# Layer 1 of a two-layer decoder: ten shared heads moved beside the last tile's chain, fp8 rounding moved to earlier steps

## The reference

```python
qkv = x @ W_qkv.T + b_qkv                       # causal attention, 16 heads of 16, B = 8, S = 128
x4 = layernorm(x + (softmax(mask(q k^T / 4)) v) @ W_out.T + b_out)
q = fq_sym((x4 @ Wq + bq) * 0.25)               # per row and head: round(q / s) * s, s = max|q| / 127
attn = fq_unsigned(softmax(q k^T))              # every head: all 1024 rows against all 1024 keys
x5 = layernorm(x4 + (attn @ v) @ Wp + bp)
wq = w.astype(float8_e4m3fn)                    # gate, up and down weights
out = layernorm(x5 + (silu(x5 @ wq_gate * s) * (x5 @ wq_up * s)) @ wq_down * s)
```

## Time and profile before

| | us |
|---|---|
| median of 3 runs | 1417.89 (1417.55 to 1419.35) |
| profiled execution, its own time | 1417.26 |
| its span | 1415.5 |
| first pass, steps 2 to 8 | about 1004.5 to 1124.8 |
| from there to head 0's reduction | 1124.8 to 1144.6 |
| SP's transposes, first and last start | 1147.5 and 1347.8 |
| feed-forward part to the end | 1347 to 1415.5 |

### The profile page before, as it was taken

How to read it: one execution, slowest core, us unless ns; L and a number is a source line. 1 busy time by engine, 2 the same in 40 slices (tenths; PEclk the granted TensorE clock), 3 DMA queues, 4 the chain that set the end, 5 groups by cost and what they waited for, 6 DMA issues and landing times.

```text
span 1415.5 us, 24455 instructions
## 1 busy us (share of the span) xinstructions
PE 1237.8 (87%) x9108; PEld 850.1 (60%) x9113; DVE 1046.5 (74%) x2349; ACT 675.3 (48%) x1286; POOL 135.1 (10%) x223
## 2 busy tenths in 40 slices
PE   6979999999999999999899999989899746677686
PEld 3747666766766766766676676656777623333344
DVE  6778578588677767858857775744888788889877
ACT  2336435434533633643553363442444358878751
POOL 2210010010011001002001100000000011111101
PEclk9989999999999999999999999999999955555588
DMA  7331002000100200200010013000300179989910
GB/s 240 154 105 63 12 12 66 13 1 16 63 12 16 62 12 12 66 12 5 26 49 12 12 63 120 20 23 24 78 8 9 31 124 167 173 151 181 166 23 30
DMA packets 176117, 86.06 MB, mean 61 GB/s; under 512 B 138240, under 2 KB 170368, under 8 KB 175744
## 3 DMA queue, kind: packets, MB, share of 16 engines
q1 hardware_dynamic: 174848, 84.13, 25.3%
q10 hardware_dynamic: 1152, 0.36, 0.1%
HBM read 43.57 MB, written 5.24 MB: 34 GB/s over the span
## 4 chain that ended last, share of the span: by engine, by line
PE 63%; DVE 19%; ACT 6%; issue 6%; DMA 5%; POOL 1%; SPq 0%; DVEq 0%; POOLq 0%; ACTq 0%
PE ps_t L1890 12%; PE ps_p L1874 11%; PE ps_s L2123 8%; PE ps_o L2040 5%; DMA w_moe<-w_moe 4%; PE ps_o L2030 4%; PE ps_o L1955 4%; PE ps_o L2123 3%; PE ps_p L1932 3%; DVE probs L1275 2%; ACT w_moe L1116 2%; PE ps_s L1932 2%; PE ps_o L1959 2%; DVE w_moe L1778 2%; DVE row_max L1281 1%
## 5 line engine op out<-in xcount | busy, mean ns | idle before, releaser
L1890 PE MATMUL ps_t<-ident,probs 128*128 128x128 f32 x1072 | 170.3, 280 | 28.5 <-ACT probs L1065 8.0
L925 ACT ACTIVATE probs<-probs 128x512 f32<-128x512 f32 x184 | 115.6, 628 | 136.6 <-DVE probs L1275 136.6
L1890 PEld LDWEIGHTS ps_t<-ident,probs 128*128 128x128 f32 x1072 | 123.2, 142 | 78.1 <-issue 37.9
L887 ACT ACTIVATE probsT<-ps_t 128x512 f32<-128x512 f32 x232 | 136.5, 589 | 64.0 <-PE ps_t L1890 63.8
L2123 PE MATMUL ps_s<-w_moe,xbT 128*128 128x352 f32 x352 | 122.1, 471 | 0.0
L1874 PE MATMUL ps_p<-w_qkv,xinT 128*128 128x512 f32 (+1 forms) x240 | 104.8, 560 | 11.4 <-DMA xinT<-in_xT 7.6
L2399 PEld LDWEIGHTS ps_p<-vals,w_moe 128*128 128x128 f16 x1024 | 37.2, 105 | 97.7 <-DMA w_moe<-w_moe 76.4
L831 POOL TENSOR_TENSOR rms<-mean_sq,neg_half 128x8 f32<-128x8 f32 x40 | 67.1, 1679 | 267.3 <-DVE mean_sq L1309 267.3
L887 ACT ACTIVATE bigT<-ps_t 128x512 f32<-128x512 f32 (+1 forms) x128 | 69.0, 553 | 33.3 <-PE ps_t L1890 31.4
L2399 PE MATMUL ps_p<-vals,w_moe 128*128 128x16 f16 x1024 | 48.2, 176 | 38.6 <-DMA w_moe<-w_moe 37.9
L2123 PEld LDWEIGHTS ps_s<-w_moe,xbT 128*128 128x128 f32 x352 | 64.0, 194 | 22.1 <-issue 1.5
(11 more groups left out here) (342 smaller groups left out, 2736.5 us busy)
## 6 DMA issues: line engine op xcount, KB each, us to landing
w_out<-in_wT_out SPq DMA_DIRECT2D x8, 2048.0 KB, 8.4
w_moe<-in_wT_gu SPq DMA_DIRECT2D x1, 5632.0 KB, 17.6
w_moe<-in_wT_down SPq DMA_DIRECT2D x1, 2816.0 KB, 10.2
keys<-keys2T SPq DMA_DIRECT2D x8, 256.0 KB, 2.0
keys2T<-keys SPq DMA_DIRECT2D x4, 512.0 KB, 10.4
w_moe<-w_moe SPq DMA_TRANSPOSE x128, 3.3
w_qkv<-in_wT_qkv SPq DMA_DIRECT2D x3, 512.0 KB, 4.9
w_qkv<-in_wT_qkv SPq DMA_DIRECT2D x1, 1536.0 KB, 8.3
```

What stands on the lines that cost most here:

```text
L887: nc.scalar.activation(dst, src.bitcast(BF16) if dst.dtype == BF16 else src, ACT.Copy)\
L925: nc.scalar.activation(probs[:, at % 4, :], probs[:, at % 4, :], ACT.Exp).then_inc(L0.exped, 1)
L1890: ins = nc.tensor.transpose(dst[:, i * P:(i + 1) * P], src(i), ident_b[:] if bf else ident[:])
```

## The change

- `STEPS_A` becomes 9: steps 9 and 10 are gone, and what they did for tile 7 stands in the loop over the heads.
- The nine fp8 pieces go to steps 1 to 8: one a step, and two in step 5.
- Heads 0 to 9 (`HEAD_START`) alternate between `ps_s` and `ps_o` and wait for exp u - 2, while `ps_t` serves tile 7's turns; from head 10 on the three pairs go round from `ps_t`, with the wait for exp u - 3.
- PE: behind head 0's scores the turn `o1` of tile 7 and `qs` of tile 6, behind head 1's the out1 projection, behind head 3's the turn `x4`, behind head 4's the q2 projection, behind head 8's the turn `qs` of tile 7. DVE, ACT and POOL have their parts at matching heads; `queries` is split into three.
- SP: the swaps of tiles 3, 4, 6 and 7 are issued inside its loop at u = 10, behind the wait for exp 10 and ahead of transpose 10.
- The first gate and up block waits for exp 125 instead of 126, the second for 126 instead of 127.

```diff
-STEPS_A = TILES + 3
+STEPS_A = TILES + 1
+HEAD_START = 10
...
-ROUND_FROM = 2
-assert ROUND_FROM + len(PIECES) <= STEPS_A
+ROUND_AT = {i: PIECES[i - 1:i] for i in range(1, 5)} | {5: PIECES[4:6]} | {i: PIECES[i:i + 1] for i in range(6, 9)}
...
-            return (ps_s, ps_o, ps_t)[u % 3]
+            return (ps_s, ps_o)[u % 2] if u < HEAD_START else (ps_t, ps_s, ps_o)[(u - HEAD_START) % 3]
...  SP
-            sp.wait_ge(L1.proj, L1.p.done(0, ("q2", LAST)))
-            for t in (3, 4, 6, 7):
-                swap_halves(t)
             for u in range(TILES * H1):
                 sp.wait_ge(exp2, u + 1)
+                if u == HEAD_START:
+                    sp.wait_ge(L1.proj, L1.p.done(0, ("q2", LAST)))
+                    for n in (3, 4, 6, 7):
+                        swap_halves(n)
...  POOL
-            for t in range(TILES):
+            for t in range(LAST):
                 power1(N4, t)
...
+                if u == 1:
+                    power1(N4, LAST)
...  ACT
+            turned("o1", LAST, lane_of(LAST).attT, D)
+            turned("qs", LAST - 1, stackTs[:, LAST - 1])
             for u in range(TILES * H1):
                 t, h = u // H1, u % H1
+                if u == 3:
+                    turned("x4", LAST, lane_of(LAST).x4T, D)
+                if u == 8:
+                    turned("qs", LAST, stackTs[:, LAST])
                 act.wait_ge(max2_ready, u + 1)
...  DVE
+            take(LAST)
             for u in range(TILES * H1):
...
+                if u == 1:
+                    norm_in(N4, LAST, "out1", xins[LAST % XINS], more=b_out1)
+                if u == 2:
+                    norm_out(N4, LAST, x4s[:, LAST])
+                if u == 4:
+                    queries_scaled(LAST)
+                if u == 5:
+                    queries_rounded(LAST)
+                if u == 6:
+                    queries_stacked(LAST)
...  PE
-                    pe.wait_ge(exp2, HEADS - 1 + b)
+                    pe.wait_ge(exp2, HEADS - 2 + b)
...
-                    if u >= 3:
+                    if 2 <= u < HEAD_START:
+                        pe.wait_ge(exp2, u - 1)
+                    if u > HEAD_START:
                         pe.wait_ge(exp2, u - 2)
...
+                    if u == 0:
+                        pe.wait_ge(taken1, TILES)
+                        turn("o1", LAST, lambda k: lane_of(LAST).att[:, k * P:(k + 1) * P], KD)
+                        queries_turned(LAST - 1)
+                    if u == 1:
+                        turned("o1", LAST)
+                        project(L1, ("out1", LAST), lane_of(LAST).attT, w_out1, 0, D)
+                    if u == 3:
+                        pe.wait_ge(N4.x_ready, TILES)
+                        turn("x4", LAST, lambda k: x4s[:, LAST, k * P:(k + 1) * P], KD)
+                    if u == 4:
+                        turned("x4", LAST)
+                        project(L1, ("q2", LAST), lane_of(LAST).x4T, w_q2, 0, D)
+                    if u == 8:
+                        queries_turned(LAST)
```

More of the change, by code:

```diff
@@ L215, in transposes1 @@
     keys = []
-    for i in range(STEPS_A):
+    for i in range(STEPS_A + 2):
         p, s, q, r = at_a(i)
@@ L508, in shared_scores @@
         def shared_scores(u):
-            return (ps_s, ps_o, ps_t)[u % 3]
+            return (ps_s, ps_o)[u % 2] if u < HEAD_START else (ps_t, ps_s, ps_o)[(u - HEAD_START) % 3]
         def block_banks(b):
-            return ps_s if b % 2 == 0 else ps_o
+            return (ps_s, ps_o)[b % 2]
         def last_sums(d):
@@ L1687, in add_bias, with queries_scaled @@
                                         heads(b_qkv1[:, D * i:D * (i + 1)], H1), ALU.add).then_inc(L1.proj_taken, 1)
-            def queries(q):
+            def queries_scaled(q):
                 lane, q2s = lane_of(q), q2ss[:, q]
@@ L1696, in queries, with queries_rounded @@
                 link1(nc.vector.tensor_reduce(q2s[:, 0, :], heads(q2, H1), X, ALU.max, apply_absolute_value=True))
+            def queries_rounded(q):
+                q2s, q2 = q2ss[:, q], lane_of(q).q2
                 link1(nc.vector.tensor_scalar(q2s[:, 0, :], q2s[:, 0, :], 1.0 / 127.0, 1e-8, ALU.mult, ALU.max))
@@ L1701, in queries, with queries_stacked @@
                 link1(nc.vector.tensor_scalar(q2, q2, ROUND, ROUND, ALU.add, ALU.subtract))
+            def queries_stacked(q):
+                lane, q2s = lane_of(q), q2ss[:, q]
+                q2 = lane.q2
                 link1(nc.vector.tensor_scalar(q2, q2, 127.0, -127.0, ALU.min, ALU.max))
@@ L1706, in queries @@
                 ins.then_inc(q2_ready, 1)
+            def queries(q):
+                queries_scaled(q)
+                queries_rounded(q)
+                queries_stacked(q)
             for i in range(STEPS_A):
@@ L1736, in _ @@
                     nc.vector.tensor_scalar(vals2[:].bitcast(FP16), values, 127.0, -127.0, ALU.min, ALU.max).then_inc(v_quantised, 1)
-                if ROUND_FROM <= i < ROUND_FROM + len(PIECES):
-                    round_fp8(*PIECES[i - ROUND_FROM])
+                for piece in ROUND_AT.get(i, ()):
+                    round_fp8(*piece)
                 if q is not None:
@@ L2328, in _, with queries_turned @@
             pe.wait_ge(v_quantised, 3)
-            pe.wait_ge(L1.shifted, TILES * G1)
-            pe.wait_ge(taken1, TILES)
             HEADS = TILES * H1
+            def queries_turned(n):
+                pe.wait_ge(q2_ready, n + 1)
+                turn("qs", n, lambda j: lane_of(n).stack[:, 2 * j:2 * j + 2, :].rearrange("p a b -> p (a b)"), 8, bf=True)
             def out_turn(n):
@@ L2377, in _ @@
                     own, other = (w.rearrange("p (a b) -> p a b", a=8) for w in (stackTs[:, t], swapped[t]))
-                    if u == 2:
+                    if u == 0:
+                        pe.wait_ge(L1.shifted, TILES * G1)
+                    if u == 1:
+                        pe.wait_ge(taken1, TILES)
+                    if u == HEAD_START:
                         turned("qs", LAST)
-                    if u >= 3:
+                    if 2 <= u < HEAD_START:
+                        pe.wait_ge(exp2, u - 1)
+                    if u > HEAD_START:
                         pe.wait_ge(exp2, u - 2)
```

## The result

The changed kernel took 1421.43 us (median of 7 runs, 1419.47 to 1424.81) against 1417.73 of the kernel before on the same chip: ratio 1.0029, 95% interval [1.0018, 1.0039]. By the medians it is 3.7 us slower. (The ratios here are estimated from all the runs of both kernels, and need not be the quotient of the medians, which is 1.0026 here.) That lies inside the range of the prediction (1413.5 to 1422.5), but the likeliest direction, "no change", was wrong: the loss is just over the 0.2% that can be told apart.

What follows compares the result with a forecast made beforehand. The prediction took a DVE, ACT and PE chain to pace the first pass and SP's issue of transposes the second from head 6 to 28. Pieces +5.5, earlier transpose 10 -4.0, tail -0.6 gave +0.9: 1418.5 us, "no change", range 1413.5 to 1422.5.

Steps and rivals of the forecast that it cites:

- the term for the fp8 pieces: First pass: an added piece lengthens DVE's list by 3.03 us in step 1 and 2.49 in step 5, +5.5 us.
- rival 1: Swaps between transposes 9 and 10 cost 1.28 us each, 10.2 instead of 5.0, giving 1423.7 us; chance 0.15.
- The swaps: Second pass, between transposes 9 and 10: eight swaps hold SP, which paces the pass, for 5.0 us.
- Rival 2: Second pass: SP's list has room, so the swaps are covered, 5.0 us less, 1413.5 us; chance 0.12.
- The head start: Handover to the second pass: heads run beside tile 7's work, so exp 10 ends 6.6 us earlier.
- Rival 1's neighbour: Handover: a head start some 3 us shorter than worked out, giving 1421.5 us; chance 0.06.
- the shift stays until the end: Second pass from head 10: SP is back to back, so transpose 10's shift, 4.0 us earlier, lasts to the pass's end.
- The tail: End of the second pass: the first gate and up block needs exp 125, not 126, and starts earlier, -0.6 us.
- Rival 3: First pass: other slack swallows both added fp8 pieces, 5.5 us less, 1413.0 (one of them, about 1415.7); chance 0.08.
- Rival 4: Handover: the clock stays high for two projections and four groups of turns, saving some 2.5 us, 1416.0; chance 0.09.

Runs made afterwards that it cites:

- E3: The changed kernel with twelve useless matmuls on PE ahead of the turn `o1` in steps 2 and 6: 1417.17 us, ratio 1.0005 to the kernel before.
- E5: The kernel before with only its eight swaps moved between transposes 9 and 10: 1421.19 us, ratio 1.0026.
- E2: The changed kernel with the swaps of tiles 3, 4, 6, 7 moved ahead of SP's wait for exps 30, 46, 62, 78: 1416.65 us, ratio 0.9999.
- E7: The changed kernel with the first two gate and up blocks waiting for one exp more, as before: 1421.42 us, ratio 1.0026.
- E8: The changed kernel run again as it is, for a second profile on the same chip: 1422.39 us, ratio 1.0025.
- E9: As E6, but one fp8 piece in step 0 and only one left for the second pass, as halves in tiles 1 and 2: 1405.08 us, ratio 0.9918.
- E1: The changed kernel with one fp8 piece a step in steps 2 to 8, the last two only converted to bf16 in the second pass: 1411.47 us, ratio 0.9965.
- E6: The changed kernel, one piece a step in steps 2 to 8, two as halves in the second pass, swaps as in E2: 1407.86 us, ratio 0.9922.
- E10: E9 with twelve useless matmuls ahead of tile 7's turn `o1` at head 0 of the second pass: 1403.99 us, ratio 0.9912.
- E4: The kernel before with only the nine fp8 pieces moved to steps 1 to 8, steps 9 and 10 kept: 1423.58 us, ratio 1.0052.

## Why the prediction was partly right

**The step that failed is the term for the fp8 pieces**, "First pass: +5.5 us", which measured 8.75 (its upper bound was 6.1). Its mechanism (DVE's list grows and nothing covers it) was right: with the clock held E3 gives 5.85, step 1 exactly its 3.03 and the doubled step 2.82, not 2.49, as only 0.2 of the wait of 0.54 was swallowed. What was missing is a second effect: a piece more on DVE makes PE idle 3.2 us, the clock falls, and the step loses time to slow projections, 2.2 us in the doubled step, and in step 1 and the one behind it 0.6 together (3.65 against 3.03). The prediction had the evidence: the same idle of 3.15 us and the fall to half stood in its own rows of the handover, and it used them for the handover alone. With 8.75 the sum would have been +4.2 and the forecast 1421.7; measured 1421.43. That the time still lay inside the range was luck: the range reached up to 1422.5 to take in part of rival 1, dear swaps, and they were not dear.

**The swaps** held: 5.06 against 5.0. E5 alone costs 3.7 us of time and 4.5 of place. Rival 1 (dear beside transposes, 1.28 each) falls: 0.63 each, gap included, right behind transpose 9. Rival 2 (covered) falls at this place. With it falls, for these transposes, the rule of the Trainium skill (DMA: Bandwidth & Descriptors, "Issuing engines are not separate DMA queues") that the time to start a DMA is usually small beside the DMA: here it is 1.28 us to issue and 3.3 to land, and the issue is what paces the pass. E2 shows both sides: the same eight DMAs are free where SP waits for exps.

**The head start** held in size. Predicted end of transpose 9 on SP: 1153.9 - 985.25 = 168.65 us behind the norm. Measured in the changed kernel, less the growth of the first pass: 1161.75 - 985.02 - 8.75 = 167.98. Rival 1's neighbour (a head start 3 us shorter) falls. From transpose 10 on nothing is won or lost (183.04 to 184.91 in every kernel; the scatter of 1.9 us is not explained), so within it the step "the shift stays until the end" stands.

**The tail**, -0.6, can't be confirmed: the block starts earlier as the prediction said, but E7 and E8 agree within their intervals.

**Rival 3** (the pieces are swallowed) falls for steps 1 and 5, and E9 shows that it would have been right for step 0, whose wait of 2.81 us is in no row that the prediction looked at. **Rival 4** (the clock holds through the handover) came out half: in the changed kernel the clock fell, came back for 3.4 us and fell again, with next to no effect (transpose 9 ends on SP 168.0 us behind the norm there, 168.2 in E1, where the clock stayed down). In E6, E9 and E10 it held through the out1 projection, and there transpose 9 ends on SP 166.5 us behind the norm. That is 1.7 to 1.8 earlier than in E1, which has the same first pass, and where the clock fell 1.4 us ahead of the turn. The turn `o1` and the out1 projection in E1 and then in E6:

```profile
1129.75 0.69 PE L1927 MATMUL ps_t<-ident,kdup 128*128 128x128 f32 x2 [3.23 <-DVE kdup L1689]
...
1131.76 2.08 PE L1911 MATMUL ps_p<-w_qkv,kdup 128*128 128x256 f32 x4
```

```profile
1128.11 0.44 PE L1928 MATMUL ps_t<-ident,kdup 128*128 128x128 f32 x2 [3.24 <-DVE kdup L1691]
...
1129.24 1.13 PE L1912 MATMUL ps_p<-w_qkv,kdup 128*128 128x256 f32 x4
```

That is what the rival meant, at 1.7 us where it had 2.5. Up to transpose 9 E1 and E6 have the same instructions in the same order, so the program is not what makes the difference up to there, and the clock is the one that the profiles show; but it is read from single profiles, and no run changed the clock there on purpose. Why the fall comes before the turn in the one and 5.3 us behind it in the other, after the same 3.2 us of idle, stays open. The Trainium skill (TensorE: Matmul & The Clock Gate, "What's actually happening") says that the gate's monitor runs freely and so the moment of a change varies from run to run; no run here tests that.

In places of transpose 10 the parts are: pieces +8.75, swaps +5.06, head start -9.6 (168.0 - 177.6, the end of transpose 9 against before's), sum +4.2. They are read from the same profile as the +4.22, so that they add up proves nothing. Other kernels bear out each: E3 splits the first, E2 has the second (5.06), and E6, without the first two, comes at -11.1, which is the head start and the 1.5 us that go with the clock's later fall there. Adding E4 and E5 (+5.8, +4.5) to E6 would give -0.9 and not +4.2: what the two pieces gone from steps 9 and 10 give back, 2.7 us in E4, would be counted twice, the 1.5 us once too often, and E5's swaps moved transpose 10 by 4.5 and not 5.06.

## What to carry to other kernels

Where an engine's list grows in a software-pipelined loop, look at what its late result makes TensorE do: an idle stretch as long as one that already lowers the granted clock elsewhere in the same profile can cost twice, once as the delay and once as the slow matmuls behind it. It need not: in E6 and E9 as long a stretch did not lower the clock. Small extra work goes where its engine waits for the pipeline to fill, or among later iterations, and not one step further on. And when the engine that issues DMAs paces a pass, every DMA of its list costs its issue time, unless it stands where that engine waits.

## What the runs showed of the hardware

- PE idle for 3.1 to 3.2 us inside the dense first pass lowered the granted clock from 1.0 to 0.5 for 3.4 to 6.8 us in all five kernels that have the doubled piece and no filling (after, E2, E4, E7, E8), though PE was busy 6.0 of 6.8 us meanwhile. Twelve matmuls that nobody reads prevented it (E3). At the handover the same idle, 3.2 us, was followed by a fall at or ahead of the next turn in the changed kernel, E1 and E3, and by none for 5.3 us in E6 and E9.
- A DMA transpose of 128x1024 elements of 16 bits holds SP's queue for 1.28 us, a plain swap for 0.6, and 7 to 12 of the 128 transposes of each profile for 1.5 to 2.9. The last is not explained.
- The end of layer 0, untouched, moved by 4.1 us between profiles (983.55 to 987.65), more than the effect that was looked for.
